# The key/value loop of a linear attention kernel, taken two token tiles at a time instead of one

## The reference

```python
Q, K, V = x @ wq.T, x @ wk.T, x @ wv.T           # wq, wk, wv: (64, 1024)
energy  = K.T @ V                                # (64, 64), a sum over all 16384 tokens
context = Q @ energy * sqrt(3 / 64)
x = layernorm(x + context @ wo.T)                # wo: (1024, 64)
h = silu(x @ w1.T * s1) * (x @ w2.T * s2)        # w1, w2: (4096, 1024)
h = gelu(h @ h1.T * sh1)                         # h1, h2: (4096, 4096)
h = gelu(h @ h2.T * sh2)
x = layernorm(x + h @ w3.T * s3)                 # w3: (1024, 4096)
```

## Time and profile before

| | us |
|---|---|
| median of 3 runs | 3417.33 |
| lowest and highest of them | 3415.44, 3419.16 |
| the profiled execution, its own time | 3417.33 |
| its span on the slowest core (core 1) | 3415.8 |
| spans of the eight cores | 3402.8 to 3415.8 |
| the changed loop on core 1, first load's issue to last energy matmul | 19.55 to 278.27 |

### The profile page before, as it was taken

The page is one execution under the profiler, slowest core; times in us unless marked ns, Lnnn a source line. Parts: engine busy times, 40 slices in busy tenths (PEclk is TensorE's granted clock), DMA queues, the critical chain, the costliest instruction groups (busy, mean ns, idle before and its releaser), DMA issues.

```text
span 3415.8 us, 40864 instructions; the slowest of 8 cores (3402.8 to 3415.8 us)
## 1 busy us (share of the span) xinstructions
PE 2856.9 (84%) x16601; PEld 1450.0 (42%) x16601; DVE 236.8 (7%) x513; ACT 833.0 (24%) x950; POOL 243.1 (7%) x460
## 2 busy tenths in 40 slices
PE   5673488889999989999998918989999999999990
PEld 4562244444444444444444404444444444444440
DVE  1112211100000000000000032220000000000002
ACT  4553233322222222222222223320000000000002
POOL 2220011000000000000000000000000000000000
PEclk9886799999999999999999959999999999999995
DMA  8993455446666656656665523322222212222112
GB/s 106 139 133 81 105 111 111 105 99 123 124 124 124 124 104 123 122 122 123 123 124 116 113 99 111 98 88 86 74 74 83 78 62 77 84 74 74 70 60 93
DMA packets 89173, 347.19 MB, mean 102 GB/s; under 512 B 10904, under 2 KB 10976, under 8 KB 70560
## 3 DMA queue, kind: packets, MB, share of 16 engines
q0 software_dynamic: 64800, 218.73, 35.2%
q10 hardware_dynamic: 14976, 92.28, 6.5%
q1 hardware_dynamic: 9216, 33.56, 2.8%
HBM read 361.83 MB, written 109.05 MB: 138 GB/s over the span
## 4 chain that ended last, share of the span: by engine, by line
PE 75%; ACT 6%; DMA 4%; issue 3%; DVE 3%; SPq 0%; ACTq 0%; DVEq 0%; POOL 0%; POOLq 0%
PE PA L596 30%; PE PB L596 29%; PE PT L558 4%; PE PA L499 3%; PE PA L507 3%; PE PB L507 3%; PE PB L499 3%; ACT WTB L571 2%; DMA X1R<-x 2%; ACT WTB L466 1%; DMA X1R<-x1s 1%; ACT TS L331 1%; DVE X1F L392 1%; DVE X1F L360 1%; DVE X1F L659 1%
## 5 line engine op out<-in xcount | busy, mean ns | idle before, releaser
L596 PE MATMUL PA<-HB,WTB 128*128 128x512 bf16 x2560 | 571.0, 382 | 43.4 <-ACT WTB L571 27.5
L596 PE MATMUL PB<-HB,WTB 128*128 128x512 bf16 x2560 | 567.2, 380 | 31.0 <-ACT WTB L571 31.0
L596 PE MATMUL PA<-GB,WTB 128*128 128x512 bf16 x2048 | 455.3, 381 | 29.8 <-ACT WTB L571 22.7
L596 PE MATMUL PB<-GB,WTB 128*128 128x512 bf16 x2048 | 452.4, 379 | 23.5 <-ACT WTB L571 23.5
L571 ACT COPY WTB<-PT 128x1024 bf16<-128x1024 bf16 x288 | 283.9, 1014 | 492.1 <-PE PT L558 492.1
L596 PEld LDWEIGHTS PA<-HB,WTB 128*128 128x128 bf16 x2560 | 248.7, 98 | 338.9 <-issue 54.9
L596 PEld LDWEIGHTS PB<-HB,WTB 128*128 128x128 bf16 x2560 | 247.7, 98 | 323.2 <-issue 36.1
L596 PEld LDWEIGHTS PA<-GB,WTB 128*128 128x128 bf16 x2048 | 198.3, 98 | 265.3 <-issue 36.6
L596 PEld LDWEIGHTS PB<-GB,WTB 128*128 128x128 bf16 x2048 | 198.0, 98 | 256.0 <-issue 25.8
L558 PE MATMUL PT<-IDB,WSB 128*128 128x128 bf16 x2304 | 166.3, 221 | 23.4 <-DMA WSB<-h 15.8
L499 PE MATMUL PA<-X1T,WTB 128*128 128x512 bf16 x512 | 124.2, 386 | 72.3 <-ACT WTB L466 50.5
(11 more groups left out here) (116 smaller groups left out, 1370.3 us busy)
## 6 DMA issues: line engine op xcount, KB each, us to landing
WSB<-h POOLq DMA_DIRECT2D x128, 512.0 KB, 6.6
XB<-x POOLq DMA_DIRECT2D x128, 256.0 KB, 6.1
h1t<-WTB ACTq DMA_DIRECT2D x32, 1024.0 KB, 8.6
h2t<-WTB ACTq DMA_DIRECT2D x32, 1024.0 KB, 8.5
WTB<-h1t POOLq DMA_DIRECT2D x32, 1024.0 KB, 5.1
WTB<-h2t POOLq DMA_DIRECT2D x32, 1024.0 KB, 5.1
WSB<-w POOLq DMA_DIRECT2D x64, 256.0 KB, 5.5
wt<-WTB ACTq DMA_DIRECT2D x32, 512.0 KB, 6.0
```

What stands on the lines that cost most here:

```text
L596: first=first, last=last, src_buf=src_buf: fi(t.matmul(PP[rp][:, g_i * 512:(g_i + 1) * 512], WTB[:, so * H + b * 1024 + j * 128: so * H + ...
```

## The change

The loop's index now counts pairs of tiles. One load brings two tiles (256 rows, 1 MB read, 512 KB written), with the two tiles side by side in XB, so XB's four slots become two slots of a pair. Its issue waits for the transposes of pair pp_i-2. TensorE makes the sixteen transposes of a pair, eight into PT[0] and eight into PT[1], after ScalarE has copied out both PT tensors of the pair before, and signals once at the end. ScalarE copies both, and signals once. The matmuls of pair pp_i-1 and the energy matmuls of pair pp_i-2 follow, sixteen and two of them, each group with one wait ahead of it and one signal at its end; VectorE's casts are grouped in the same way. Only two semaphores are used for the loads. Buffers have their old sizes, and nothing outside this loop is edited. (The expression `SGP[rp2] if False else SGP[r4 // 2 + 0]` is SGP[0] or SGP[1], that of the pair's slot.)

```diff
--- before.py
+++ after.py
@@ -229,65 +229,80 @@
     xb_dma = {}
     KVQP = [PP[0][:, 0:192], PP[0][:, 512:704],
             PP[1][:, 0:192], PP[1][:, 512:704]]
-    for t_i in range(NT + 4):
-        if t_i < NT:
-            r4 = t_i % 4
-            r2 = t_i % 2
-            if t_i >= 4:
-                w('g', 't', xtp[t_i - 4])
-            em('g', lambda g, t_i=t_i, r4=r4: g.dma_start(
-                out=XB[:, r4 * E:(r4 + 1) * E],
-                in_=x[t_i * 128:(t_i + 1) * 128, :]).then_inc(SGP[r4], 16))
-            xb_dma[t_i] = inc(f'g{r4}', 16)
-            w('t', f'g{r4}', xb_dma[t_i])
-            if t_i >= 2:
-                w('t', 's', xte[t_i - 2])
-            for c in range(EC):
-                em('t', lambda t, r2=r2, r4=r4, c=c: fi(t.transpose(
-                    PT[r2][:, c * 128:(c + 1) * 128],
-                    XB[:, r4 * E + c * 128: r4 * E + (c + 1) * 128], IDB[:]),
-                    c == EC - 1))
-            xtp[t_i] = inc('t')
-            w('s', 't', xtp[t_i])
-            if t_i >= 4:
-                w('s', 't', kvq[t_i - 4])
-            em('s', lambda s, r2=r2, r4=r4: s.copy(
-                XT[:, r4 * E:(r4 + 1) * E], PT[r2][:, 0:1024]).then_inc(SS, 1))
-            xte[t_i] = inc('s')
-        tj = t_i - 2
-        if 0 <= tj < NT:
-            rj = tj % 4
-            W_ = 192 if tj < OT else 128
-            w('t', 's', xte[tj])
-            if tj >= 4:
-                w('t', 'v', kve[tj - 4])
-            for c in range(EC):
-                em('t', lambda t, rj=rj, c=c, W_=W_: fi(t.matmul(
-                    KVQP[rj][:, 0:W_],
-                    XT[:, rj * E + c * 128: rj * E + (c + 1) * 128],
-                    KVQT[:, c * 192: c * 192 + W_],
-                    start=(c == 0), stop=(c == EC - 1)), c == EC - 1))
-            kvq[tj] = inc('t')
-            w('v', 't', kvq[tj])
-            if tj >= 4:
-                w('v', 't', emm[tj - 4])
-            own_ = tj < OT
-            em('v', lambda v, rj=rj, W_=W_, own_=own_: fi(v.tensor_copy(
-                KVB[:, rj * 192: rj * 192 + W_], KVQP[rj][:, 0:W_]),
-                not own_, SV))
-            if own_:
-                em('v', lambda v, tj=tj, rj=rj: fi(v.tensor_copy(
-                    QN[:, tj * D:(tj + 1) * D], KVQP[rj][:, 128:192]), True, SV))
-            kve[tj] = inc('v')
-        tk = t_i - 4
-        if 0 <= tk < NT:
-            rk = tk % 4
-            w('t', 'v', kve[tk])
-            em('t', lambda t, rk=rk, tk=tk: t.matmul(
-                PEn[:], KVB[:, rk * 192: rk * 192 + 64],
-                KVB[:, rk * 192 + 64: rk * 192 + 128],
-                start=(tk == 0), stop=(tk == NT - 1)).then_inc(ST, 1))
-            emm[tk] = inc('t')
+    NPAIR = NT // 2
+    for pp_i in range(NPAIR + 3):
+        if pp_i < NPAIR:
+            rp2 = pp_i % 2
+            r4 = rp2 * 2
+            ta = 2 * pp_i
+            if pp_i >= 2:
+                w('g', 't', xtp[pp_i - 2])
+            em('g', lambda g, ta=ta, r4=r4: g.dma_start(
+                out=XB[:, r4 * E:(r4 + 2) * E].rearrange("p (a f) -> p a f", a=2),
+                in_=x[ta * 128:(ta + 2) * 128, :].rearrange(
+                    "(a p) f -> p a f", p=128)).then_inc(SGP[rp2] if False else SGP[r4 // 2 + 0], 16))
+            xb_dma[pp_i] = inc(f'g{rp2}', 16)
+            w('t', f'g{rp2}', xb_dma[pp_i])
+            if pp_i >= 1:
+                w('t', 's', xte[pp_i - 1])
+            for ti in range(2):
+                for c in range(EC):
+                    em('t', lambda t, r4=r4, ti=ti, c=c: fi(t.transpose(
+                        PT[ti][:, c * 128:(c + 1) * 128],
+                        XB[:, (r4 + ti) * E + c * 128: (r4 + ti) * E + (c + 1) * 128],
+                        IDB[:]), ti == 1 and c == EC - 1))
+            xtp[pp_i] = inc('t')
+            w('s', 't', xtp[pp_i])
+            if pp_i >= 2:
+                w('s', 't', kvq[pp_i - 2])
+            em('s', lambda s, r4=r4: s.copy(
+                XT[:, r4 * E:(r4 + 1) * E], PT[0][:, 0:1024]))
+            em('s', lambda s, r4=r4: s.copy(
+                XT[:, (r4 + 1) * E:(r4 + 2) * E], PT[1][:, 0:1024]).then_inc(SS, 1))
+            xte[pp_i] = inc('s')
+        pj = pp_i - 1
+        if 0 <= pj < NPAIR:
+            r4j = (pj % 2) * 2
+            w('t', 's', xte[pj])
+            if pj >= 2:
+                w('t', 'v', kve[pj - 2])
+            for ti in range(2):
+                tj = 2 * pj + ti
+                W_ = 192 if tj < OT else 128
+                for c in range(EC):
+                    em('t', lambda t, r4j=r4j, ti=ti, c=c, W_=W_: fi(t.matmul(
+                        KVQP[r4j + ti][:, 0:W_],
+                        XT[:, (r4j + ti) * E + c * 128: (r4j + ti) * E + (c + 1) * 128],
+                        KVQT[:, c * 192: c * 192 + W_],
+                        start=(c == 0), stop=(c == EC - 1)),
+                        ti == 1 and c == EC - 1))
+            kvq[pj] = inc('t')
+            w('v', 't', kvq[pj])
+            if pj >= 2:
+                w('v', 't', emm[pj - 2])
+            for ti in range(2):
+                tj = 2 * pj + ti
+                own_ = tj < OT
+                W_ = 192 if own_ else 128
+                em('v', lambda v, r4j=r4j, ti=ti, tj=tj, W_=W_, own_=own_:
+                   fi(v.tensor_copy(
+                    KVB[:, (tj % 4) * 192: (tj % 4) * 192 + W_],
+                    KVQP[r4j + ti][:, 0:W_]), ti == 1 and not own_, SV))
+                if own_:
+                    em('v', lambda v, tj=tj, r4j=r4j, ti=ti: fi(v.tensor_copy(
+                        QN[:, tj * D:(tj + 1) * D],
+                        KVQP[r4j + ti][:, 128:192]), ti == 1, SV))
+            kve[pj] = inc('v')
+        pk = pp_i - 2
+        if 0 <= pk < NPAIR:
+            w('t', 'v', kve[pk])
+            for ti in range(2):
+                tk = 2 * pk + ti
+                em('t', lambda t, tk=tk, ti=ti: fi(t.matmul(
+                    PEn[:], KVB[:, (tk % 4) * 192: (tk % 4) * 192 + 64],
+                    KVB[:, (tk % 4) * 192 + 64: (tk % 4) * 192 + 128],
+                    start=(tk == 0), stop=(tk == NT - 1)), ti == 1))
+            emm[pk] = inc('t')
     barrier()
 
     em('s', lambda s: s.activation(ENF[:], PEn[:], AF.Copy, bias=0.0,
```

## The result

The changed kernel takes 3446.74 us at the median of 10 runs, beside 3418.15 us for the kernel before. The ratio is 1.0083 (95% interval 1.0059 to 1.0107), so it is slower by 0.8%, some 28 us. Forecast were 3447 us.

A forecast was written before the change was run, and what follows sets the result against it. The prediction took the loop as bound by its loads, and by their latency after the change: 26.6 us, 63 steps of 4.38 us and 5.9 us end at 308.4 us, +30 us, so 3447 us (range 3418 to 3474).

The forecast's parts named there:

- The ring gets shorter in time: XB's slots: one other load (3.9 us) instead of three (5.85 us) covers a slot's turn; 4.18 to 4.58 us a pair.
- The sum: Whole loop: 63 steps of 4.38 us a pair plus start and end, ending at 308.4 us against 278.3, +30 us.
- Start and end: Loop's edges: first transpose at about 26.7 us instead of 24.71; 5.9 us after the last landing instead of 3.4.
- The load's 6.6 us: XB's pair load, issue to landing: 6.6 us, the median of L536's loads of equal bytes.
- The engines' floor: DMA engines in the loop: a pair needs 3.9 us, with no gain per byte from a larger load.
- Two signs: DMA queue in the loop: a share near 0.87 would show the forecast right, packets shorter than 0.217 us a rival.
- rival B: XB's loads: the larger load is really cheaper, 3.6 us a pair, 19 us less, 3398 us; chance 0.08.
- Rival A: DMA engines stay the loop's bound, 3.9 to 4.0 us a pair, 3417 to at most 3424 us; chance 0.19.
- Rival C: Loop: landing takes 7.0 us and the clock stays low, 4.78 us a pair, +57 us, 3474 us; chance 0.19.

The follow-up runs named there:

- e4: The kernel before with three XB slots of one tile instead of four; ratio 1.0142 to the kernel before.
- e1: The changed kernel with four pair slots in XB instead of two; ratio 0.9919 to the kernel before.
- e5: The changed kernel with three pair slots in XB instead of two; ratio 0.9925 to the kernel before.
- e9: The changed kernel with PT's halves handed over one by one between TensorE and ScalarE, still two pair slots; ratio 1.0082 to the kernel before.
- e2: The changed kernel with one load per tile into four tile slots, compute still by pairs; ratio 1.0061 to the kernel before.
- e3: The kernel before with only the load part changed: one load for two tiles, two pair slots, compute tile by tile; ratio 1.0168 to the kernel before.
- e8: The kernel before, compute tile by tile, with one load for two tiles and four pair slots; ratio 0.9893 to the kernel before.
- e6: The kernel before with eight XB slots of one tile instead of four; ratio 0.9903 to the kernel before.
- e10: The kernel before, compute tile by tile, with one load for two tiles and eight pair slots; ratio 0.9903 to the kernel before.
- e7b: The kernel before with float32 loads from SyncE's queue into four float32 slots, VectorE casting each tile to bf16; ratio 1.0523 to the kernel before.

## Why the prediction was right, and where it wasn't

- **The ring gets shorter in time: right, and the cause.** e4 shows the effect of depth alone, e1 and e5 that more slots remove the loss, e9 that the turn-taking over PT is not the main part, and e2 and e3 that whatever makes a slot's turn longer costs time.
- **The sum, term by term.** From the first landing (27.81 us) to the last (302.98) it is 4.37 us a pair on the slowest core, where the sum had 4.38; the step between issues, 4.45 us, is longer since the second load, queued behind the first, took 11.7 us to land and the last one 6.6. The terms of a slot's turn, as means over the trace, were: landing to first transpose 0.45 us (0.15 in the sum), sixteen transposes 1.26 (1.46, the mean of its two clocks), to the issue 0.58 (0.54), issue to landing 6.54 (6.6). Together 8.83 against 8.75. So two errors nearly cancel, and that is luck. The clock was at the low level for (1 - 0.87) / 0.5 = 26% of the loop, not half, and 26% of the transposes ran at the low level's duration. And I gave nothing for the time between landing and transposes beyond the wake-up, though 18 pairs also waited for ScalarE (9.9 us). Start and end came out at 27.81 us and 6.1 us, forecast 26.6 and 5.9; the first issue of a pair kept GpSimd for 0.713 us instead of 0.537, which may be part of the later start.
- **The load's 6.6 us** was the right size by a row of another stage, and this was partly luck as well: the time depends on what else is outstanding. Pair loads took 6.4 us at the median with two outstanding, 7.7 with three (e5), 8.1 with four (e1), 10.1 with four and compute tile by tile (e8).
- **The engines' floor: wrong.** The step said that 3.9 us a pair is what the engines need, because their share was 100.0% and packets cost twice the time for twice the bytes. The rows are read rightly, but the conclusion doesn't follow: with more loads outstanding the same engines move a pair in 3.16 us, at a share of 1.07. The kernel before was bound by its depth too, as eight slots of the same load (e6) show. Two signs came out otherwise than forecast for the same reason: a share of 0.78, not 0.87, and 230 x 16 x 0.821 / 14361 = 0.210 us a packet, below the 0.217 that I had named as a sign of rival B. In e6, with the very loads of the kernel before, a packet took 140 x 16 x 1.068 / 12592 = 0.190 us. So a packet's time is no fixed price, and the sign was a poor one. The forecast survived since both cycles that it compared lay above the real limit, and since before's time per pair was measured, whatever its cause.
- **Small misreadings of rows 1.** The clock row of the kernel before is lower in slices two to five (8, 8, 6, 7), not in the first two, and the loop reaches into the fourth slice. Nothing in the sum rests on it.
- **Rival A** (the engines stay the bound at 3.9 us) is out by the share of 0.78 and by the deep rings. **Rival B** (a larger load is cheaper) is out: at equal bytes outstanding size made no difference between e6 and e8. By the same runs the Trainium skill's rule to batch to 1 MiB or more (DMA: Bandwidth & Descriptors, Bandwidth), which the prediction weighed, brings nothing here: loads of 512 KB read, eight outstanding, did as well. **Rival C** is out: the longest landing, 11.7 us, is that of the second load at the start, the mean of 6.54 us lies only 0.1 above the median, and the clock stayed higher than it assumed.

A version beats both: pair loads, four pair slots and compute tile by tile (e8), 0.9893 of the kernel before, 3373 us at the median. Eight tile slots do as well within the intervals (0.9903).

## What to carry to other kernels

Work out a buffer's full turn, from landing through its last reader and the issue to the next landing, and divide it by the number of buffers. When every buffer is always in use this equals the time per tile whatever the bound is: in e10 the terms of a turn add up to 24.9 us, an eighth of it is 3.1 us, and yet the ring wasn't the bound. It tells something before the change is made, if the load's time is taken from a lightly filled queue, and a run with one buffer more or less decides. Merging two loads into one at equal memory halves the number of buffers and makes each turn longer. Before treating a rate as a floor, look for, or make, a run with more loads outstanding; here 8 KB more per partition were worth 1%.

## What the runs showed of the hardware that I had not expected

- A DMA share near 1.00 did not mean full engines. From 60 to 200 us the share was 1.01 at 137 GB/s, 0.91 at 136 GB/s (e2) and 1.07 at 166 GB/s (e8).
- Casting loads issued from GpSimd read 332 GB/s per core on eight cores at once with 4 MB of reads outstanding (e6, e8), and no more with 8 MB (e10).
- A mean granted clock of 1.00 can stand beside transposes of the low level's duration. In the float32 kernel with the serial order (e7b) they took 311 ns each at the median, where those of the changed kernel took 219 at the median and up to 314, while the stretch says

```profile
60.00:200.00 140.00, 90.39 (x723) 76.30 (x721) 39.19 (x92) 42.56 (x42) 0.00 (x0) 1.00 0.49 158
```

No run shows why the two disagree. It is a reason to compare the durations of like instructions before trusting a mean clock.
